# Expert up products from split fp32r parts, and another order of a pair's tiles on TensorE

## The chip, the core and the metric

The kernel runs on one core of a Trainium2 chip. What counts is the device time of one launch in microseconds. The median of three runs before the change is 1347.92 us (1346.98 to 1354.15).

## What is computed

Sixteen sequences of 256 tokens with 256 features pass through three blocks, each with a layer norm ahead and a residual sum behind: attention with its own small feed-forward network, cross attention to a context with another, and a layer of eight experts. The change concerns the last one. Each token goes to the expert whose centroid is nearest, and only this expert's output is kept:

```
xn = rms_norm(x, scale)
ids = argmin(dist2(xn, centroids), axis=-1)
for e in range(8):
    h = xn @ up_w[e]            # (tokens, 256) @ (256, 1024)
    a, g = split(h, 2)
    y = (a * silu(g)) @ down_w[e]   # (tokens, 512) @ (512, 256)
    out = where(ids == e, y, out)
return out + skip
```

Everything is float32 at the ends.

## The kernel before

**Batches.** A first phase runs over the sequences as batches, five stages deep (P, A, B, D, C in `PHASES`): in one turn the stages work on five batches at once. Each engine has its own program, a function `turn(it)` that is run once for each turn, and engines meet by semaphores alone. In the last turns stages fall away: turn B + 1 has B, D and C, turn B + 2 has D and C, turn B + 3 has C alone. Stage D is the second half of cross attention's network (`D.h0` to `D.h3` and `D.out`), stage C normalises its result (`c_x2`), makes the rows for the experts (`c_rows`), stores them to `rows_x` and `rows_skip` and finds each token's expert (`nearest`). In turn B + 1 SyncE also loads the experts' weights (`load_experts`): `up`, 1 MB for each expert, and `down`, half as much.

**Routing.** When the last rows are stored, VectorE sorts the tokens by expert in a chain of some forty steps on the semaphore `s_route`, with a few products on TensorE between. It ends with `sorted_row`, the rows in order of experts, and `tile_expert`, the expert of each tile of 128 rows. There are 39 tiles.

**Tiles.** Two tiles, u = 0 and 1, make a pair k. `tile_steps` runs `step(k, n, nxt, nxt2)` on every engine: the first pair, then a hardware loop of 16 pairs, two pairs written out, and a last single tile. For each tile GpSimd gathers 128 rows (`m_in`), TensorE transposes them (`transpose_in`), ScalarE copies them to `m_xT`; TensorE makes the up product in two halves of 512 columns, two products over C = 2 chunks each (`up_half`), with the rows as the stationary operand and the expert's weights streaming; ScalarE takes SiLU of the gate half (`m_sg`), VectorE multiplies with the other (L1482, `m_h`); TensorE transposes the hidden rows (`turn_hidden`, L1869), ScalarE copies them (L878, `m_hT`), TensorE makes the down product (`down_tile`), VectorE adds the skip rows (`m_out`) and GpSimd scatters the result. TensorE reads the expert's number from `tile_expert` into a register (`value_load`, L1855) and addresses the weights by it.

TensorE's order in a pair is written by hand: the up product of tile 0, the first half of tile 1's, the transposes of tile 0's hidden rows, the second half of tile 1's up product, the down product of tile 0, the transposes of tile 1's hidden rows, the transposes of the next pair's rows, the down product of tile 1.

All products of the experts are in fp32. Other products of the kernel are already made from fp32r parts: a value is rounded to fp32r (`hi`), the rest is taken (`low`), and three passes hi.hi, hi.low and low.hi are summed.

Of the kernel before, what the change touches and what calls it, by code (L numbers as in the profile page):

```python
# [166 lines left out]
def _build(nc, d, ctx):  # L167
# [77 lines left out]

    b_kh, b_kl, b_qh, b_ql = (sbuf(ctx, name, [P, C, S], F32R) for name in ("b_kh", "b_kl", "b_qh", "b_ql"))
# [6 lines left out]
    def carver():  # L253

        at = [0]
# [21 lines left out]
    w1o = p1("w1o", [P, C, D])  # L277
    w11 = p1("w11", [P, C, HID])
    w12 = p1("w12", [P, J, D])
# [8 lines left out]

    rec = p1("rec", [P, 3, S])
    rec_few = p1("rec_few", [P, 16])  # L290
    x1 = p1("x1", [P, T, D])

    c_in = p1("c_in", [P, T, D])
    b_ctxT = p1("b_ctxT", [P, C, S])
    b_xl = p1("b_xl", [P, T, D])
    b_xT = p1("b_xT", [P, C, S])


    b_v = p1("b_v", [P, T, D])
    b_nm = p1("b_nm", [P, T, C, 4, 32])  # L300
    b_p = p1("b_p", [P, NPB, T, S])
    b_zT = p1("b_zT", [P, C, S])
    b_yT = p1("b_yT", [P, C, S])
    b_q = p1("b_q", [P, T, D])
    b_hT = p1("b_hT", [P, J, S])
# [211 lines left out]
    s_route, s_pp, s_wmoe = map(sem, ("routing_chain", "prefixes_made", "experts_loaded"))  # L517
# [13 lines left out]
    pr.close()  # L531
    up = sbuf(ctx, "up", [P, E, C, 2 * EH])
    down = sbuf(ctx, "down", [P, E, EJ, D])
    p3 = carver()
    m_row = p3("m_row", [P, 2, 2, 1], U32)
    m_token = p3("m_token", [P, 2, 1], U32)
    m_in = p3("m_in", [P, 2, D])
    m_skip = p3("m_skip", [P, 2, D])
    m_xT = p3("m_xT", [P, 2, C, P])
    m_sg = p3("m_sg", [P, 2, EH])  # L540
    m_h = p3("m_h", [P, 2, EH])
    m_hT = p3("m_hT", [P, 2, EJ, P])
    m_out = p3("m_out", [P, 2, D])
    oh = p3("oh", [P, NT, E])
    r_pp = p3("r_pp", [P, NT, E])
# [17 lines left out]
    r_id = p3("r_id", [P, 4, TILES_MAX])  # L563
# [9 lines left out]
    BY_TILE = {"m_loaded": 16, "m_skip": 16, "m_row": 1, "m_x": 1, "m_xT": 1, "m_up": 1, "m_silu": 1,  # L573
# [14 lines left out]
    PAIRS = (TILES_MAX - 1) // 2  # L588
# [3 lines left out]
    H_BANK, DOWN_BANK = (6, 2), (7, 4)  # L592

    def tile_steps(eng, body):
        body(0, 2, 2, 2)
        with eng.Fori(0, PAIRS - 3) as k:
            body(k + 1, 2, 2, 2)
        body(PAIRS - 2, 2, 2, TILES_MAX - 2 * PAIRS)
        body(PAIRS - 1, 2, TILES_MAX - 2 * PAIRS, 0)
        if TILES_MAX > 2 * PAIRS:  # L600
            body(PAIRS, 1, 0, 0)

# [4 lines left out]
    def _(sp):  # L607
# [23 lines left out]
        def load_experts():  # L631

            after(sp, "b_xl", B - 1)
            for e in range(E):
                sp.dma_start(up[:, e], w_view(d["L0_ffn_up_w"][e])).then_inc(s_wmoe, 16)
                sp.dma_start(down[:, e], w_view(d["L0_ffn_down_w"][e])).then_inc(s_wmoe, 16)
# [47 lines left out]
    def _(act):  # L684
# [29 lines left out]

        def evacuate(it, job, dst, view=None):

            src = full(act, it, job)[:]
            copy(dst, src if view is None else view(src)).then_inc(e_sem(job), 1)  # L718

        def turn(it):  # L720
# [15 lines left out]
            if Dd:  # L736
                copy(flat(d_qT_hi[:]), full(act, it, "D.q")[:]).then_inc(sig["d_qhi"], 1)
            if A:
# [65 lines left out]
            for what, st, n in PLAN:  # L804
                if st not in it.stages:
                    continue
                if what == "lengths":
                    after(act, "c_rows", c, T)
                    for t in range(T):
                        nc.scalar.activation(b_zT[:, t], c_rows[:, t, 0:D], ACT.Square,  # L810
# [18 lines left out]
            if Cc:  # L829
                for t in range(T):  # L830
                    nc.scalar.activation(c_x2[:, t], c_x2[:, t], ACT.Identity, scale=c_sc[:, 7, t:t + 1],
                                         bias=c_sc[:, 9, t:t + 1]).then_inc(sig["c_rows"], 1)
            if it.first == SPLIT_FROM - 1:
                round_aside((2,))
# [34 lines left out]
        def transposed(k, u):  # L869
            after_tile(act, "m_x", k, u)  # L870
            copy(m_xT[:, u].rearrange("p c s -> p (c s)"), bank[u][:, 0:C * P]).then_inc(mig[u]["m_xT"], 1)

        def step(k, n, nxt, nxt2):
            for u in range(n):
                after_tile(act, "m_up", k, u)
                nc.scalar.activation(m_sg[:, u], bank[3 + 2 * u][:], ACT.Silu).then_inc(mig[u]["m_silu"], 1)  # L876
                after_tile(act, "m_ht", k, u)
                copy(m_hT[:, u].rearrange("p j s -> p (j s)"), bank[H_BANK[u]][:]).then_inc(mig[u]["m_hT"], 1)  # L878
            for u in range(nxt):
                transposed(k + 1, u)  # L880
# [9 lines left out]
    def _(pool):  # L890
# [156 lines left out]

        def step(k, n, nxt, nxt2):
            for u in range(nxt2):
                after_tile(pool, "m_x", k + 1, u)  # L1050
                after_tile(pool, "m_row", k, u)
                gather(m_in, rows_x, m_row[:, 0, u], "m_loaded", u)
            for u in range(n):

                after_tile(pool, "m_out", k, u)
                pool.indirect_dma_start(
                    out=d["out"], out_offset=bass.IndirectOffsetOnAxis(ap=m_token[:, u], axis=0),
                    in_=m_out[:, u], in_offset=None, bounds_check=B * S - 1, oob_is_err=False,
                ).then_inc(mig[u]["m_stored"], 16)
                if u < nxt:  # L1060
                    gather(m_skip, rows_skip, m_row[:, 1, u], "m_skip", u)
# [9 lines left out]
    def _(dve):  # L1071
# [101 lines left out]
        def turn(it):  # L1173
# [155 lines left out]
            if it.first == SPLIT_FROM:  # L1329
                for name in SPLIT[::2]:  # L1330
                    dve.wait_ge(s_low_out[name], 16)
            if Dd:
# [612 lines left out]
```

## Time and profile before

| | us |
|---|---|
| median of three runs | 1347.92 |
| profiled execution | 1350.49 |
| its span, first to last instruction | 1348.8 |
| batches, to 1013 | 1013.0 |
| drain and routing, to the first up product | 72.5 |
| experts, to the end | 263.3 |

The stages are cut by hand at the start of turn B + 2's work and at the first up product. In the profile's rows PE is TensorE, PEld its weight loads, DVE VectorE, ACT ScalarE, POOL GpSimd and SP SyncE; a time is counted from the span's start. An fp32 product appears as two records. The idle time in square brackets is that of the engine just before the row, with what ended it; "issue" means that the engine waited for nothing that the profile shows.

### The profile page before, as it was taken

The page shows a single profiled execution, that of the slowest core. Times are in us where ns is not written, and L with a number is a line of the kernel's source. Part 1 is how long each engine was busy: PE and PEld are TensorE (multiplying, and loading weights), DVE is VectorE, ACT ScalarE, POOL GpSimd, SP SyncE. Part 2 cuts the span into 40 slices and gives each one's busy share as a digit, 9 for nine tenths or more (in the row PEclk, how much of TensorE's full clock was granted, in tenths as well). Part 3 has the DMA queues.
Part 4 walks back from the last instruction along what each step waited for, and adds up shares of the span by engine and source line. Part 5 has one row for each costly group of instructions (what it writes and reads, how often), then busy time and mean ns, then how long its engine had stood idle before and what let it go on. Part 6 is the DMA issues. An engine that isn't in the chain of part 4 may idle for free.

```text
span 1348.8 us, 29314 instructions
## 1 busy us (share of the span) xinstructions
PE 1223.9 (91%) x9542; PEld 915.5 (68%) x9543; DVE 811.2 (60%) x2110; ACT 611.4 (45%) x1288; POOL 413.7 (31%) x712
## 2 busy tenths in 40 slices
PE   6497999999999999999999999999985289999997
PEld 4274778778787877878787787878765145555554
DVE  3737667777786877778687777877644611211211
ACT  3426456464746646474654647465442122222211
POOL 1310324233142423314142331414122234444352
PEclk9598999999999999999999999999998589999998
DMA  8402520303213030321303032130383012121121
GB/s 265 126 1 110 222 107 17 111 16 109 80 52 117 16 109 16 109 80 48 121 16 109 16 109 77 48 124 9 111 324 113 16 49 64 51 62 53 55 66 28
DMA packets 51768, 112.29 MB, mean 83 GB/s; under 512 B 7333, under 2 KB 38863, under 8 KB 44944
## 3 DMA queue, kind: packets, MB, share of 16 engines
q1 hardware_dynamic: 45456, 96.81, 21.3%
q0 software_dynamic: 5616, 14.43, 3.6%
q10 hardware_dynamic: 656, 0.52, 0.1%
q8 instruction: 24, 0.39, 0.1%
q14 instruction: 16, 0.13, 0.0%
HBM read 89.72 MB, written 22.94 MB: 84 GB/s over the span
## 4 chain that ended last, share of the span: by engine, by line
PE 76%; DVE 10%; ACT 6%; issue 5%; DMA 2%; POOL 1%; SPq 0%; DVEq 0%; ACTq 0%; POOLq 0%
PE bank L1505 69%; PE bank L1540 3%; DVE a_p L1295 2%; PE bank L1706 2%; ACT shared L823 2%; PE bank L1869 1%; DMA rows_skip<-shared 1%; ACT shared L878 1%; ACT a_p L818 1%; DVE b_ql L1199 1%; DVE a_split L1227 1%; DVE a_split L1226 1%; DVE a_split L1225 1%; DVE a_ss L1236 1%; ACT a_sq L741 1%
## 5 line engine op out<-in xcount | busy, mean ns | idle before, releaser
L1505 PE MATMUL bank<-shared 128*128 128x256 f32 (+4 forms) x1730 | 320.3, 376 | 27.6 <-POOL shared L1030 11.3
L1505 PEld LDWEIGHTS bank<-shared 128*128 128x128 f32 (+2 forms) x1730 | 219.8, 166 | 88.7 <-issue 31.7
L1295 DVE TENSOR_TENSOR a_p<-a_p,eb 128x385 f32<-128x385 f32 x256 | 125.9, 555 | 75.6 <-ACT a_p L818 75.6
L1505 PE MATMUL bank<-up,shared 128*128 x312 | 143.8, 604 | 11.1 <-issue 11.1
L991 POOL TENSOR_SCALAR a_rz<-a_ms 128x2 f32<-128x2 f32 x16 | 3.1, 191 | 407.5 <-ACT a_sq L842 407.5
L818 ACT ACTIVATE a_p<-bank 128x385 f32<-128x385 f32 x256 | 105.1, 504 | 44.3 <-PE bank L1505 44.2
L1482 DVE TENSOR_TENSOR shared<-bank,shared 128x512 f32<-128x512 f32 x39 | 27.0, 692 | 153.7 <-ACT shared L876 153.7
L1505 PEld LDWEIGHTS bank<-up,shared 128*128 128x128 f32 x312 | 56.9, 192 | 75.6 <-issue 75.6
L876 ACT ACTIVATE shared<-bank 128x512 f32<-128x512 f32 x39 | 23.3, 597 | 137.2 <-PE bank L1505 137.2
L1505 PE MATMUL bank<-down,shared 128*128 x312 | 76.8, 390 | 7.2 <-ACT shared L878 7.2
L823 ACT ACTIVATE shared<-bank 128x512 f32<-128x512 f32 x128 | 66.1, 603 | 35.3 <-PE bank L1505 35.3
L1262 DVE TENSOR_REDUCE shared<-bank 128x2 f32<-128x512 f32 x128 | 79.4, 684 | 1.3 <-PE bank L1505 1.3
L1505 PEld LDWEIGHTS bank<-down,shared 128*128 128x128 f32 x312 | 58.2, 192 | 27.2 <-issue 20.9
L971 POOL TENSOR_TENSOR a_split<-a_sq,a_split 128x256 f16<-128x256 f32 x64 | 42.8, 699 | 104.6 <-ACT a_split L772 104.6
L1035 POOL DMA_INDIRECT shared<-rows_x,shared x35 | 33.1, 945 | 112.1 <-PE bank L1844 107.0
L1505 PE MATMUL bank<-a_p,a_v 128*32 128x256 f32 (+1 forms) x1024 | 58.5, 347 | 8.0 <-DVE a_p L1295 6.2
L1505 PE MATMUL bank<-w_low,a_hT_hi 128*128 128x256 f32 x224 | 63.4, 283 | 0.0
L1505 PE MATMUL bank<-w_hi,a_hT_hi 128*128 128x256 f32 x224 | 62.9, 281 | 0.0
L1505 PE MATMUL bank<-d_qT_hi,w_hi 128*128 128x256 f32 x256 | 57.4, 306 | 5.8 <-DVE d_qT_low L1122 5.8
L1505 PE MATMUL bank<-w_hi,a_hT_low 128*128 128x256 f32 x224 | 62.4, 279 | 0.0
L1505 PE MATMUL bank<-w0qk,a_xnT 128*128 128x512 f32 x128 | 61.1, 621 | 0.7 <-ACT a_xnT L718 0.7
L927 POOL TENSOR_TENSOR shared<-shared,mhalf 128x2 f32<-128x2 f32 x80 | 56.3, 704 | 12.7 <-POOL shared L959 6.6
(237 smaller groups left out, 2724.8 us busy)
## 6 DMA issues: line engine op xcount, KB each, us to landing
w_low<-low_w SPq DMA_DIRECT2D x44, 1024.0 KB, 4.8
up<-in_L_ffn_up_w SPq DMA_DIRECT2D x8, 1024.0 KB, 13.9
x_in<-in_x SPq DMA_DIRECT2D x16, 256.0 KB, 2.7
shared<-in_ctx SPq DMA_DIRECT2D x16, 256.0 KB, 3.1
rows_x<-shared SPq DMA_DIRECT2D x16, 256.0 KB, 5.8
rows_skip<-shared SPq DMA_DIRECT2D x16, 256.0 KB, 6.2
down<-in_L_ffn_down_w SPq DMA_DIRECT2D x8, 512.0 KB, 12.3
toep<-a_hT SPq DMA_DIRECT2D x1, 3072.0 KB, 10.2
```

Of the source, the lines that this page charges most:

```text
L818: nc.scalar.activation(a_p[:, head % NPA], ps[:, 0:SCOLS], ACT.Exp).then_inc(e_sem(f"A.s{head}"), 1)
L823: nc.scalar.activation(b_p[:, head % NPB].rearrange("p t s -> p (t s)"), ps[:], ACT.Exp).then_inc(e_sem(f"B.s{head}"), 1)
L876: nc.scalar.activation(m_sg[:, u], bank[3 + 2 * u][:], ACT.Silu).then_inc(mig[u]["m_silu"], 1)
L927: pool.tensor_tensor(out, in_, mhalf[:, 0:out.shape[-1]], ALU.pow).then_inc(sig[name], 1)
L971: ins = pool.tensor_tensor(a_split[:, t, H0:, slot, :], hat[:, H0:], a_split[:, t, H0:, 0, :], ALU.subtract)
L1035: pool.indirect_dma_start(out=dst[:, u], out_offset=None, in_=src.ap(), in_offset=bass.IndirectOffsetOnAxis(ap=rows, axis=0)).then_inc(mig ...
L1262: dve.tensor_reduce(b_nm[:, n // 4, :, n % 4, 0:1], ps[:].rearrange("p (m s) -> p m s", s=S), AX_X, ALU.max, negate=True).then_inc(e_sem(f ...
L1295: tt(a_p[:, n_ % NPA], a_p[:, n_ % NPA], eb[:, n_], ALU.mult).then_inc(sig["a_p"], 1)
L1482: tt(m_h[:, u], bank[2 + 2 * u][:], m_sg[:, u], ALU.mult).then_inc(mig[u]["m_h"], 1)
L1505: return mm(out, lhsT=lhsT, rhs=rhs, start=first, stop=last, **kw)
L1540: ins = nc.tensor.transpose(ps[:, c * S + t * P:c * S + (t + 1) * P], x[:, t, c * P:(c + 1) * P], ident[:])
L1706: ins = nc.tensor.transpose(ps[:, g * P:(g + 1) * P], a_split[:, t, h:h + 2].rearrange("p h s d -> p (h s d)"), ident16[:])
```

## The change

**Up products.** `up_half` makes six products instead of two: m_xhi with up_hi, m_xhi with up_low, m_xlow with up_hi, each over two chunks, all in fp32r. ScalarE's copy of the transposed rows now writes m_xhi in fp32r, and VectorE gets a new step for each tile, `rest_of_rows`, which subtracts it from the transposed rows in PSUM and writes m_xlow.

**Weights.** `up_hi` is made by ScalarE (`round_up_weights`, eight casts of 128x2048) and `up_low` by VectorE (`rest_of_up`, sixteen subtracts of 128x1024, in place of `up`). ScalarE makes experts 0 to 2 in turn B + 2 after the cast of D.q, 3 to 6 after the same turn's C rows, and 7 once VectorE has taken D.out. VectorE makes the parts of experts 0 to 3 in turn B + 2 before it takes D.out, 4 and 5 after the statistics of c_x2, 6 and 7 at the end of the routing chain. TensorE waits for all of them before the first transposes of rows. Each expert's load has a semaphore of its own. `up_hi` lies where tensors of the first phase lay, and these are laid out in another order.

**Order in a pair.** On TensorE: the whole up product of tile 0, the down product of tile 1 of the pair before, the transposes of tile 0's hidden rows, the transposes of the next pair's tile 0, the whole up product of tile 1, the down product of tile 0, the transposes of tile 1's hidden rows, the transposes of the next pair's tile 1. The expert of the tile before is loaded once more at a pair's start. The other engines' steps follow this order. Two pairs are written out ahead of the loop now, which has 15 turns. Rows of both tiles share bank 0, the down products bank 7.

```diff
+        def round_up_weights(which):
+            for e in which:
+                act.wait_ge(s_up[e], 16)
+                copy(flat(up_hi[:, e]), flat(up[:, e])).then_inc(s_up_hi, 1)
...
+        def rest_of_up(halves):
+            for n in halves:
+                e, c_ = n // C, n % C
+                if c_ == 0:
+                    dve.wait_ge(s_up_hi, e + 1)
+                ins = tt(up_low[:, e, c_], up[:, e, c_], up_hi[:, e, c_].bitcast(F32), ALU.subtract)
+            ins.then_inc(s_up_low, len(halves) // C)
...
+            if it.first == B + 2:
+                rest_of_up(range(0, 8))
             if Dd:
                 ps = full(dve, it, "D.out")
...
+            if it.first == B + 2:
+                rest_of_up(range(8, 12))
...
+        rest_of_up(range(12, 16))
+
+        def rest_of_rows(k, u):
+            after_tile(dve, "m_xT", k, u)
+            tt(flat(m_xlow[:, u]), x_bank(u), flat(m_xhi[:, u]).bitcast(F32), ALU.subtract
+               ).then_inc(mig[u]["m_xl"], 1)
...
-            def up_half(u, half):
-                for c in range(C):
-                    w = up[:, bass.ds(expert[u], 1), c, half * EH:(half + 1) * EH]
-                    ins = product(bank[2 + 2 * u + half][:], m_xT[:, u, c], w.rearrange("p o n -> p (o n)"),
-                                  c == 0, c == C - 1)
+            def up_half(u, half, x_low_new):
+                for x, w_part in ((m_xhi, up_hi), (m_xhi, up_low), (m_xlow, up_hi)):
+                    if x is m_xlow and x_low_new:
+                        after_tile(pe, "m_xl", k, u)
+                    for c in range(C):
+                        w = w_part[:, bass.ds(expert[u], 1), c, half * EH:(half + 1) * EH]
+                        ins = product(bank[2 + 2 * u + half][:], x[:, u, c], w.rearrange("p o n -> p (o n)"),
+                                      c == 0 and x is m_xhi and w_part is up_hi, c == C - 1 and x is m_xlow)
                 return ins
...
+            choose(0, 2 * k)
+            if further:
+                choose(-1, 2 * k - 1)
+            up_tile(0)
+            if further:
+                down_tile(1, 1)
             if n == 2:
+                choose(1, 2 * k + 1)
             turn_hidden(0)
+            if nxt > 0:
+                transpose_in(k + 1, 0)
             if n == 2:
+                up_tile(1)
+            down_tile(0, 0)
             if n == 2:
                 turn_hidden(1)
-            for u in range(nxt):
-                transpose_in(k + 1, u)
-            if n == 2:
-                down_tile(1)
+            if nxt > 1:
+                transpose_in(k + 1, 1)
```

TensorE at the end of the pair loop, before (ISA rows set addresses, TENSOR_LOAD reads an expert's number; the rows behind the branch are the next pair, and a loop turn begins with the same two loads):

```order
L1505 ISA
L1505 MATMUL bank<-down,shared 128x256
L596 REGISTER_ALU
L596 COMPARE_AND_BRANCH
L1855 TENSOR_LOAD tile_expert
L1855 ISA x2
L1855 TENSOR_LOAD tile_expert
L1855 ISA x2
L1505 ISA [waits m_hT1,m_h0,m_xT0]
L1505 MATMUL bank<-up,shared 128x512
```

The same place after:

```order
L1962 MATMUL bank<-ident,shared 128x128 [waits m_hT1,m_h1]
L1962 MATMUL bank<-ident,shared 128x128 x3
L1929 MATMUL bank<-ident,shared 128x128 [waits m_xl0,m_loaded1]
L1929 MATMUL bank<-ident,shared 128x128
L616 REGISTER_ALU
L616 COMPARE_AND_BRANCH
L1940 TENSOR_LOAD tile_expert
L1940 ISA x2
L1940 TENSOR_LOAD tile_expert
L1940 ISA x2
L1589 ISA [waits m_h0,m_xT0]
L1589 MATMUL bank<-up_hi,m_xhi 128x512
```

The down products of tile 1 stood between the last wait and the branch; now the transposes of tile 1's hidden rows and of the next rows stand there.

VectorE in turn B + 2, from the end of `nearest` (CAST expert_of) to the statistics of stage D's result, before (L1335 takes D.out):

```order
L1194 CAST expert_of<-shared 128x2 [waits c_index]
L1335 TENSOR_TENSOR shared<-bank,shared 128x512 [waits b_qb2,bank_full5]
L1134 BN_STATS shared<-shared 128x6 [waits bank_free5]
L1134 BN_STATS shared<-shared 128x6
L1137 BN_AGGR shared<-shared 128x2 [waits c_stats] x2
```

After, from the last of the eight subtracts on (L1390 takes D.out):

```order
L1163 TENSOR_TENSOR up_low<-up,up_hi 128x1024 [waits up_weights_rounded]
L1163 TENSOR_TENSOR up_low<-up,up_hi 128x1024
L1390 TENSOR_TENSOR shared<-bank,shared 128x512 [waits b_qb2,bank_full5]
L1187 BN_STATS shared<-shared 128x6 [waits bank_free5]
L1187 BN_STATS shared<-shared 128x6
L1190 BN_AGGR shared<-shared 128x2 [waits c_stats] x2
```

Eight rows like the first two stand between the CAST and the row that takes D.out.

VectorE at the end of turn B + 2, from the statistics of c_x2 to the first step of turn B + 3, which waits for GpSimd's chain of norms, before:

```order
L1134 BN_STATS shared<-shared 128x6 [waits c_x2]
L1134 BN_STATS shared<-shared 128x6
L1137 BN_AGGR shared<-shared 128x2 [waits c_stats2] x2
L1269 SCALAR_TENSOR_TENSOR shared<-shared 128x256 [waits c_norms]
L1269 SCALAR_TENSOR_TENSOR shared<-shared 128x256
```

After, from the last row of the statistics on:

```order
L1190 BN_AGGR shared<-shared 128x2 [waits c_stats2] x2
L1163 TENSOR_TENSOR up_low<-up,up_hi 128x1024 [waits up_weights_rounded]
L1163 TENSOR_TENSOR up_low<-up,up_hi 128x1024
L1163 TENSOR_TENSOR up_low<-up,up_hi 128x1024 [waits up_weights_rounded]
L1163 TENSOR_TENSOR up_low<-up,up_hi 128x1024
L1322 SCALAR_TENSOR_TENSOR shared<-shared 128x256 [waits c_norms]
```

Four subtracts stand between the statistics, for which GpSimd's chain of norms waits, and the step that waits for this chain.

## Rows read from the trace of the kernel before

**Rows 1.** Busy time in two stretches (stretch, us, busy by engine, granted clock, DMA).
```profile
1013.00:1085.50 72.50, 27.97 (x160) 22.65 (x158) 34.79 (x96) 13.02 (x31) 21.94 (x43) 0.67 0.16 58
1085.50:1348.80 263.30, 239.60 (x854) 141.79 (x854) 50.27 (x189) 57.06 (x116) 109.92 (x113) 0.98 0.18 53
```

**Rows 2.** Timeline, TensorE, one pair in the loop (start, duration, work, idle before).
```profile
1283.67 5.41 PE L1505 MATMUL bank<-up,shared 128*128 x12 [0.63 <-issue]
1288.92 0.60 PE L1869 MATMUL bank<-ident,shared 128*128 128x128 f32 x4
1289.36 1.88 PE L1505 MATMUL bank<-up,shared 128*128 x4
1291.08 1.89 PE L1505 MATMUL bank<-down,shared 128*128 x8
...
1294.16 1.99 PE L1505 MATMUL bank<-down,shared 128*128 x8 [0.33 <-ACT shared L878]
1296.79 5.41 PE L1505 MATMUL bank<-up,shared 128*128 x12 [0.64 <-issue]
```

**Rows 3.** Timeline, TensorE, fp32r products of batch work, eight steps apart.
```profile
560.06 0.28 PE L1505 MATMUL bank<-w_hi,a_hT_hi 128*128 128x256 f32 x1
...
561.00 0.28 PE L1505 MATMUL bank<-w_hi,a_hT_low 128*128 128x256 f32 x1
```

**Rows 4.** Timeline of a pair's second half: products, multiply, weight loads (PEld).
```profile
1107.42 1.89 PE L1505 MATMUL bank<-down,shared 128*128 x8
...
1108.25 0.69 DVE L1482 TENSOR_TENSOR shared<-bank,shared 128x512 f32<-128x512 f32 x1 [3.18 <-ACT shared L876]
...
1108.99 0.51 PEld L1869 LDWEIGHTS bank<-ident,shared 128*128 128x128 f32 x4
...
1110.50 1.59 PEld L1505 LDWEIGHTS bank<-down,shared 128*128 128x128 f32 x8 [0.56 <-issue]
...
1113.19 0.30 PEld L1505 LDWEIGHTS bank<-up,shared 128*128 128x128 f32 x2 [1.10 <-issue]
```

**Rows 5.** Timeline, TensorE, written-out pairs and the last tile.
```profile
1319.92 1.99 PE L1505 MATMUL bank<-down,shared 128*128 x8 [0.33 <-ACT shared L878]
1321.91 5.41 PE L1505 MATMUL bank<-up,shared 128*128 x12
...
1340.66 3.15 PE L1505 MATMUL bank<-down,shared 128*128 x8 [0.76 <-ACT shared L878]
```

**Rows 6.** Timeline, TensorE's weight loads before the first up product.
```profile
1083.83 0.29 PEld L1844 LDWEIGHTS bank<-ident,shared 128*128 128x128 f32 x2 [0.79 <-DMA shared<-rows_x,sorted_row]
...
1085.49 0.50 PEld L1505 LDWEIGHTS bank<-up,shared 128*128 128x128 f32 x2 [1.37 <-issue]
```

**Rows 7.** Groups by shape: cast and subtract of 2048 columns (busy us, mean ns).
```profile
L713 ACT CAST made<-w 128x2048 fp32r<-128x2048 f32 x1 | 1.9, 1930 | 0.0
...
L1111 DVE TENSOR_TENSOR made<-w,made 128x2048 fp32r<-128x2048 f32 x1 | 2.3, 2325 | 1.2 <-DMA rounded_w<-made 1.2
```

**Rows 8.** Loads of up weights: last issue (SyncE), and sizes, us to landing.
```profile
1002.38 3.26 SPq L635 DMA_DIRECT2D up<-in_L_ffn_up_w  x1
...
up<-in_L_ffn_up_w SPq DMA_DIRECT2D x8, 1024.0 KB, 13.9
```

**Rows 9.** Timeline of the drain: ScalarE once, VectorE twice.
```profile
1027.36 0.47 ACT L754 ACTIVATE shared<-bank,shared 128x256 f32<-128x256 f32 x1 [8.12 <-PE bank L1505]
...
1041.38 0.69 DVE L1335 TENSOR_TENSOR shared<-bank,shared 128x512 f32<-128x512 f32 x1 [4.22 <-PE bank L1505]
...
1050.68 0.88 DVE L1269 SCALAR_TENSOR_TENSOR shared<-shared 128x256 f32<-128x256 f32 x2 [3.80 <-POOL shared L955]
```

**Rows 10.** Timeline of the drain, GpSimd and VectorE at the same time.
```profile
1027.47 1.31 POOL L980 TENSOR_TENSOR shared<-shared 128x512 f32<-128x512 f32 x1
...
1027.55 2.96 DVE L1269 SCALAR_TENSOR_TENSOR shared<-shared 128x256 f32<-128x256 f32 x2 [3.20 <-POOL shared L955]
```

More of the change, by code:

```diff
@@ L737, in turn @@
                 copy(flat(d_qT_hi[:]), full(act, it, "D.q")[:]).then_inc(sig["d_qhi"], 1)
+            if it.first == B + 2:
+                after(act, "x1_kept", B - 1)
+                round_up_weights(range(3))
             if A:
@@ L832, in turn @@
                                          bias=c_sc[:, 9, t:t + 1]).then_inc(sig["c_rows"], 1)
+            if it.first == B + 2:
+                after(act, "c_nx", c)
+                round_up_weights(range(3, E - 1))
+                taken(act, it, "D.out")
+                round_up_weights(range(E - 1, E))
             if it.first == SPLIT_FROM - 1:
@@ L1046, in _, with store, next_rows @@
             gather(m_in, rows_x, sorted_row[:, 2 + u:3 + u], "m_loaded", u)
-        def step(k, n, nxt, nxt2):
[L1049 to L1061, printed above, removed]
+        def store(k, u, n, more):
+            after_tile(pool, "m_out", k, u, n)
+            pool.indirect_dma_start(
+                out=d["out"], out_offset=bass.IndirectOffsetOnAxis(ap=m_token[:, u], axis=0),
+                in_=m_out[:, u], in_offset=None, bounds_check=B * S - 1, oob_is_err=False,
+            ).then_inc(mig[u]["m_stored"], 16)
+            if more:
+                gather(m_skip, rows_skip, m_row[:, 1, u], "m_skip", u)
+        def next_rows(k, u):
+            after_tile(pool, "m_x", k + 1, u)
+            after_tile(pool, "m_row", k, u)
+            gather(m_in, rows_x, m_row[:, 0, u], "m_loaded", u)
+        def step(k, n, nxt, nxt2):
+            if not isinstance(k, int) or k > 0:
+                store(k, 1, 0, n == 2)
+            if nxt2 > 0:
+                next_rows(k, 0)
+            store(k, 0, 1, nxt > 0)
+            if nxt2 > 1:
+                next_rows(k, 1)
         tile_steps(pool, step)
@@ new lines, in next_row, with hidden_tile, sum_out @@
+        def next_row(k, u):
+            after_tile(dve, "m_loaded", k + 1, u)
+            ts(m_row[:, 0, u], of_tile(3, 2 * k + 4 + u), 1.0, None, ALU.mult).then_inc(mig[u]["m_row"], 1)
+        def hidden_tile(k, u):
+            after_tile(dve, "m_silu", k, u)
+            tt(m_h[:, u], bank[2 + 2 * u][:], m_sg[:, u], ALU.mult).then_inc(mig[u]["m_h"], 1)
+        def sum_out(k, u, back, more):
+            after_tile(dve, "m_stored", k, u, -back)
+            ts(m_token[:, u], of_tile(2, 2 * k + u - 2 * back), 1.0, None, ALU.mult)
+            after_tile(dve, "m_down", k, u, 1 - back)
+            after_tile(dve, "m_skip", k, u, 1 - back)
+            if more:
+                ts(m_row[:, 1, u], of_tile(3, 2 * k + 2 + u - 2 * back), 1.0, None, ALU.mult)
+            tt(m_out[:, u], down_bank(u), m_skip[:, u], ALU.add).then_inc(mig[u]["m_out"], 1)
```

189 lines of the change are left out of this document (101 added, 88 removed).

## The prediction

> **What bounds the kernel now.** I read the busy time by stage first, then TensorE's rows of one pair of tiles, then the rows of the stage between the last batch and the first tile. From 1085.50 on, the experts take 263.30 us and TensorE is busy for 239.60 of them at a granted clock of 0.98, while VectorE is busy for 50.27 and ScalarE for 57.06 [rows 1]: this stage is TensorE's, and shorter products there shorten it. The 72.50 us before it (the drain) are different: TensorE is busy for 27.97, VectorE for 34.79, no engine is full [rows 1], and the end is set by a chain of small dependent steps in which VectorE takes part. Work added there on VectorE costs time wherever it outlasts VectorE's wait.
>
> A pair takes 1296.79 - 1283.67 = 13.12 us [rows 2]. The reader is to see two holes in it: 0.33 us before the second down product (waiting for ScalarE's copy) and 0.64 us, called issue, before the next pair. An up product of 512 columns is two records of 0.43 us (1.72 us for four, from 1289.36 to 1291.08), so a tile's four take 3.44; a down product of a tile takes the same 1.72, four transposes 0.44 (1288.92 to 1289.36) [rows 2].
>
> **The up products.** They go from four fp32 products to twelve fp32r products of 512 columns a tile. The trace has fp32r products of 256 columns only: eight steps from 560.06 to 561.00 are 0.1175 us each [rows 3]. For 512 columns the upper bound is twice that, 0.235. The lower one is half an fp32 record of the same 512 columns, 0.215 [rows 2]. A part of the 0.1175 may belong to the instruction and not to its columns, and no row tells how much, so I take the middle, 0.225: 12 x 0.225 = 2.70 us a tile against 3.44. The bounds are 2.58 and 2.82.
> The 256-column step is longer than a rule gives: the Trainium skill, "TensorE: Matmul & The Clock Gate", section "Back-to-back issue gap", states N/2.4 + 2.5 ns, thus 109 ns for 256 columns and 216 for 512, and does not speak of fp32r. The row's 117.5 decides for 256. An estimate by that page's 216 ns would make a tile 2.59 us and the whole kernel some 4 us shorter than my sum.
>
> **The order in a pair.** A whole up product now stands ahead of the down product of the tile before it, and this covers the way from an up product through SiLU and the multiply to the transposes of the hidden rows: its end at 1107.42, VectorE's multiply at 1108.25, the weight load of the transposes at 1108.99, thus 1.57 us [rows 4], under a down product of 1.72. That hole stays closed, and the 0.33 us before the second down product goes, since the copy of m_hT has a whole up product as cover.
>
> What is late next is the pair's end. The 0.64 us there is not TensorE's array but its sequencer: released at 1110.50 by m_hT, it issues four down products, the branch and two loads of an expert's number, and only 2.69 us later, at 1113.19, the next up product's weights [rows 4]. Where the steps are written out without a loop, the down product starts at 1319.92 and the up product at 1321.91, 1.99 apart instead of 2.63 with no idle left [rows 5]: the branch is worth 0.64, and the two loads hide only because 1.72 us of down products are queued behind the wait. In the new order the last wait before the branch is on m_h of tile 1, and behind it are queued only its four transposes and two of rows, 0.44 + 0.22 = 0.66 us. So from the end of the second up product it takes 1.57 to the wait's release and then some 2.69 (six transposes for four down products, the rest the same): 4.26 us, where the array has 1.72 + 0.66 = 2.38 to do. The hole at the pair's end grows from 0.64 to 1.88 us.
> The third load of an expert's number stands behind the down product of the tile before, which the sequencer issues early since its waits are long over; I cost it at nothing, and at up to 0.83 us a pair if that is wrong (two loads with two transposes take 1085.49 - 1083.83 = 1.66 [rows 6]).
>
> A pair in the loop after: 2.70 + 1.72 + 0.66 + 2.70 + 4.26 = 12.04, against 13.12: 1.08 x 15 loop turns = 16.2 us. The new step 1 is written out and takes 12.04 - 0.64 = 11.40 against 13.12; the two pairs after the loop take 11.40 against some 12.4: 1.7 + 2.0 = 3.7. The first pair has two shorter up products (2 x 0.74 = 1.5), the single last tile one (0.74), and its down product, which took 3.15 us instead of 1.99 with TensorE idle before it [rows 2, 5], should lose these 1.16, since the down product of the tile before now fills that idle time: 3.4 together. Sum of the experts' stage: **23.3 us saved**. VectorE and ScalarE get one subtract and none respectively more per tile; at a fifth of their time busy [rows 1] this costs nothing, and GpSimd's six transfers a pair keep their number.
>
> **The drain.** Eight casts of 128x2048 at 1.93 us on ScalarE, sixteen subtracts of 128x1024 on VectorE, each half of 2.33, so 1.17 us [rows 7]. The last load of up weights is issued at 1002.38 and a load lands 13.9 us after its issue [rows 8], before any of them is needed. Three casts (5.8 us) go into ScalarE's idle 8.12 us that end at 1027.36 [rows 9]: nothing. The other five follow the C rows, when ScalarE waits anyway: nothing, else a few us if VectorE had to wait for one.
> The subtracts come in three places. Eight stand ahead of the add that takes D.out: 9.4 us where VectorE idled 4.22 [rows 9]: **+5.2**. Behind them wait that add, the statistics and everything to the routing. Four come after the statistics of x2: 4.7 us where VectorE idles 3.80 [rows 9], at least +0.9. But GpSimd runs its ten-step chain of norms in that idle time, and the trace shows the two in each other's way: two VectorE operations with both inputs in SBUF took 2.96 us while GpSimd multiplied rows from SBUF [rows 10], and the same two 0.88 at 1050.68 without [rows 9]. If the four and the chain can't overlap, it costs all 4.7; I take **+4.4**. The last four follow sorted_row and TensorE waits for them before the first transposes: from 1079.3 to 1084.0, then rows 0, their low part, rows 1 and one load; the first transposes of the second rows stood at 1083.83 [rows 6]. I count **+1.3** at the first up product, and up to +5.3 if GpSimd's gathers and the subtracts hold each other up.
> The Trainium skill's "SBUF — State Buffer", section "Who interferes with whom", agrees with the rows at 1027.55 (a VectorE instruction with two SBUF inputs contends with a GpSimd one that reads SBUF), but infers that a tensor_tensor does not hold up the writing of descriptors. By this rule the gathers run on and the 5.3 falls away; no row of before shows it.
> Sum of the drain: 5.2 + 4.4 + 1.3 = **10.9 us lost**, bounds 7.4 and 15.2.
>
> **Sum.** The profiled execution took 1350.49 us (span 1348.8), 2.6 above the median 1347.92; the sum is made in its rows: 1350.49 - 23.3 + 10.9 = 1338.1, and against the median 1335.5. With the bounds of the product (4.7 us either way over 39 tiles) and of the drain this case reaches from 1327 to 1345.
>
> **The rivals.**
> *The hole at the pair's end does not grow*, because the sequencer gets through loads and branch faster when it isn't behind products. For it: the hole is only 0.64 now. Against it: 2.69 us from release to load with nothing else to do [rows 4]. It gives 1.24 us back in each of 19 pairs, 23.6: 1312.
> *The third load is not covered*: 0.83 x 19 = 15.8 us more: 1351, no change. For it: loads are long [rows 6]; against it: the down product before it has no open wait.
> *Slower: the sequencer can't feed the array.* Each up tile needs twenty sequencer steps now (twelve products, eight address steps) against eight. From 1110.50 to 1113.19 it made seventeen in 2.69 us, 0.16 each [rows 4]; at that price a tile takes 3.2 us instead of 2.70, over 39 tiles 19.5 us more: 1355. It turns the gain into a loss from 3.02 us a tile on. Against it: those seventeen hold the loads and the branch, and fp32r products with fixed addresses come every 0.1175 [rows 3].
> *Slower: the clock falls in the hole.* After the idle times of the last tile the down product ran 3.15 us against 1.99 [rows 2, 5]. If each of 19 holes did that, it would cost 1.16 x 19 = 22: 1357. Against it: a hole of 1.88 us stands between stretches without idle time, while there two lay close together.
>
> **How the numbers follow.** Forecast 1335.5 with chance 0.61; the hole that doesn't grow 0.13; the third load 0.14; fed too slowly 0.08; clock 0.04. Half a per cent, what a measurement of this kernel can tell from no change, is 6.7 us: 1341.2 to 1354.7. Of the forecast's own range about a sixth lies above 1341.2. Faster 0.51 + 0.13 = 0.64; same 0.10 + 0.14 = 0.24; slower 0.12. The range runs from 1312 to 1352, leaving out half of the first rival and the two slower ones, under 2 in 10.
>
> **What would show it.** In the loop, twelve up products in 2.6 to 2.8 us, no idle time before the hidden transposes, an issue hole of 1.7 to 2.0 us before each pair and a pair of 11.8 to 12.3. In the drain, the add of D.out some 5 us later, GpSimd's chain of norms stretched, the first up product some 11 us later. An issue hole under 1 us or up products over 3 us a tile would make the prediction wrong.

## The result, and the profile after

The changed kernel takes 1334.95 us (median of 4 runs, 1334.41 to 1335.46), the kernel before 1347.45 on the same chip (1346.82 to 1354.15): 12.5 us by the two medians. The ratio of the runs is 0.9888 (95% interval 0.987 to 0.9906), which is 15.1 us (12.7 to 17.5). The medians probably understate the gain: in the experiments below, the kernel before has medians of 1349.1 to 1350.5 from 7 to 11 runs. The forecast was 1335.5. The profiled execution took 1335.46 (span 1333.7), 15.0 less than that of before, which was 3 us above its own median; the traces are compared with each other below, stage by stage, since the batches' work ahead of the drain differs by several us between executions.

The two stretches of [rows 1], at the same times after the change (stretch, us, busy by engine, granted clock, DMA):

```profile
1013.00:1085.50 72.50, 27.27 (x156) 22.89 (x156) 46.50 (x101) 26.31 (x36) 20.14 (x38) 0.67 0.15 56
1085.50:1334.00 248.50, 209.23 (x1017) 173.56 (x1014) 73.29 (x240) 58.30 (x118) 116.18 (x117) 0.97 0.20 58
```

VectorE's busy time in the drain rose from 34.79 to 46.50 us, ScalarE's from 13.02 to 26.31: the splitting of the weights. The drain now ends at 1095.18, so the second row still holds its last 9.7 us. In the experts' stage alone, from 1095.18 on, TensorE is busy for 207.72 of 238.52 us: its work fell from 239.60, but it is idle for 30.8 us where it was idle for 23.7. What it waits for there, after and (second fence) before (waited for, us in total, times, longest):

```profile
PE bank L1589 <- issue: 24.2, 20, 1.4
...
PE bank L1589 <- ACT shared L913: 0.8, 1, 0.8
```
```profile
PE bank L1505 <- issue: 11.1, 18, 1.0
PE bank L1505 <- ACT shared L878: 7.2, 20, 0.8
```

The 20 waits for ScalarE's copy are gone all but the last one, and the idle time called issue has more than doubled. One pair in the loop, which answers to [rows 2] (TensorE: start, duration, work, idle before; then weight loads, PEld, of its second half):

```profile
1203.62 0.73 PE L1589 MATMUL bank<-up_hi,m_xhi 128*128 x2 [1.41 <-issue]
...
1206.46 1.89 PE L1589 MATMUL bank<-down,shared 128*128 x8
1208.18 0.60 PE L1962 MATMUL bank<-ident,shared 128*128 128x128 f32 x4
1208.62 0.38 PE L1929 MATMUL bank<-ident,shared 128*128 128x128 f32 x2
1208.76 0.71 PE L1589 MATMUL bank<-up_hi,m_xhi 128*128 x2
1209.31 0.63 PE L1589 MATMUL bank<-up_low,m_xhi 128*128 x2
...
1211.61 1.89 PE L1589 MATMUL bank<-down,shared 128*128 x8
...
1215.57 0.72 PE L1589 MATMUL bank<-up_hi,m_xhi 128*128 x2 [1.42 <-issue]
```
```profile
1213.18 0.51 PEld L1962 LDWEIGHTS bank<-ident,shared 128*128 128x128 f32 x4
1213.66 0.25 PEld L1929 LDWEIGHTS bank<-ident,shared 128*128 128x128 f32 x2
1215.57 0.32 PEld L1589 LDWEIGHTS bank<-up_hi,m_xhi 128*128 128x128 f32 x2 [1.65 <-issue]
```

The pair takes 1215.57 - 1203.62 = 11.95 us (13.12 before). Twelve up products take 2.85 (1208.76 to 1211.61): two of 512 columns every 0.46, but the first two 0.55. No idle time stands before the transposes of the hidden rows, and one hole of 1.41 ends the pair.

The drain, VectorE, then GpSimd, which answers to [rows 9, 10]:

```profile
1037.62 9.17 DVE L1163 TENSOR_TENSOR up_low<-up,up_hi 128x1024 fp32r<-128x1024 f32 x8
1046.70 0.69 DVE L1390 TENSOR_TENSOR shared<-bank,shared 128x512 f32<-128x512 f32 x1
...
1052.12 4.60 DVE L1163 TENSOR_TENSOR up_low<-up,up_hi 128x1024 fp32r<-128x1024 f32 x4
1058.93 0.88 DVE L1322 SCALAR_TENSOR_TENSOR shared<-shared 128x256 f32<-128x256 f32 x2 [2.21 <-POOL shared L990]
...
1087.58 4.63 DVE L1163 TENSOR_TENSOR up_low<-up,up_hi 128x1024 fp32r<-128x1024 f32 x4
```
```profile
1052.29 1.10 POOL L968 TENSOR_SCALAR shared<-shared 128x2 f32<-128x2 f32 x1 [2.80 <-DVE shared L1190]
1053.47 1.53 POOL L962 TENSOR_TENSOR shared<-shared,mhalf 128x2 f32<-128x2 f32 x1
1055.08 0.55 POOL L972 TENSOR_TENSOR shared<-shared 128x2 f32<-128x2 f32 x1
1055.71 1.06 POOL L974 TENSOR_TENSOR shared<-shared 128x2 f32<-128x2 f32 x1
...
1087.85 2.08 POOL L1070 DMA_INDIRECT shared<-rows_x,sorted_row  x1 [6.52 <-DVE sorted_row L1530]
1090.24 1.67 POOL L1070 DMA_INDIRECT shared<-rows_x,sorted_row  x1 [0.31 <-issue]
```

VectorE no longer idles ahead of the D.out add. Beside four subtracts the first four steps of GpSimd's chain of norms took 1.10, 1.53, 0.55 and 1.06 us (0.22, 0.70, 0.20 and 0.20 before), and the two gathers beside the last four took 2.08 and 1.67 (1.25 and 0.96 before). The first up product follows at 1095.18.

To compare drains whatever came before them, I count from VectorE's subtract of D's q, a step that the change left as it was (before at 1023.67, after at 1024.24). Added by the change: 4.75 us up to the D.out add (17.71 to 22.46), 2.93 from there to the last batch's rows (9.30 to 12.23), nothing in the routing, 1.42 from the list of rows to the first up product (6.40 to 7.82): 9.1. From the first up product to the end: 263.3 us before, 238.5 after, 24.8 saved.

### The profile page after: what moved, and what is told of

Its sections match the earlier page's. It is cut to its first block, busy times and chain, and to the rows that moved or that the text cites. A ratio compares the mean times of both kernels' runs of the same rounds, so it can differ in the third digit from the quotient of the medians.

```text
span 1333.7 us, 29945 instructions
## 1 busy us (share of the span) xinstructions
PE 1192.6 (89%) x9698; PEld 948.7 (71%) x9699; DVE 846.5 (63%) x2165; ACT 625.9 (47%) x1296; POOL 417.6 (31%) x712
## 4 chain that ended last, share of the span: by engine, by line
PE 75%; DVE 11%; issue 6%; ACT 5%; DMA 2%; POOL 1%; SPq 0%; DVEq 0%; ACTq 0%; POOLq 0%
PE bank L1589 67%; PE bank L1624 3%; DVE a_p L1348 2%; PE bank L1790 2%; ACT shared L852 2%; PE bank L1962 1%; DVE up_low L1163 1%; DMA rows_skip<-shared 1%; ACT a_p L847 1%; PE bank L1929 1%; DVE b_ql L1252 1%; DVE a_split L1279 1%; DVE a_split L1280 1%; DVE a_ss L1289 1%; DVE a_split L1278 1%
## 5 line engine op out<-in xcount | busy, mean ns | idle before, releaser
L911 ACT ACTIVATE shared<-bank 128x512 f32<-128x512 f32 x39 | 23.3, 597 | 113.0 <-PE bank L1589 113.0
L1589 PE MATMUL bank<-up_hi,m_xhi 128*128 x156 | 53.1, 422 | 24.2 <-issue 24.2
L1589 PE MATMUL bank<-down,shared 128*128 x312 | 73.8, 379 | 0.8 <-ACT shared L913 0.8
L1086 POOL DMA_INDIRECT out_rows<-shared x39 | 39.5, 1012 | 98.0 <-DVE shared L1562 90.7
L962 POOL TENSOR_TENSOR shared<-shared,mhalf 128x2 f32<-128x2 f32 x80 | 57.2, 715 | 12.7 <-POOL shared L994 6.6
L882 ACT ACTIVATE a_hT_hi<-bank 128x512 fp32r<-128x512 f32 x56 | 33.5, 598 | 52.9 <-PE bank L1589 52.9
## 6 DMA issues: line engine op xcount, KB each, us to landing
down<-in_L_ffn_down_w SPq DMA_DIRECT2D x8, 512.0 KB, 12.4
toep<-a_hT SPq DMA_DIRECT2D x1, 3072.0 KB, 10.2
```

Of the source, the lines that this page charges most:

```text
L882: nc.scalar.activation(flat(a_hT_hi[:, 2 * n:2 * n + 2]), ps[:], ACT.Relu).then_inc(sig["a_hhi"], 1)
L962: pool.tensor_tensor(out, in_, mhalf[:, 0:out.shape[-1]], ALU.pow).then_inc(sig[name], 1)
L1086: pool.indirect_dma_start(out=d["out"], out_offset=bass.IndirectOffsetOnAxis(ap=m_token[:, u], axis=0), in_=m_out[:, u], in_offset=None, b ...
L1589: return mm(out, lhsT=lhsT, rhs=rhs, start=first, stop=last, **kw)
```

## The experiments

A turning is the transposes of a tile's hidden rows h; the loop's turn is the branch back to its head. Theory S: TensorE's sequencer makes the hole at the pair's end. The last wait ahead of the branch and the two loads of expert numbers is answered late, and little is queued behind it. Rival A: the hole is a wait for another engine. For the drain, theory D: the 9 us are subtracts in VectorE's chain; theory C: subtracts and GpSimd's work slow each other.

**The turned loop.** TensorE's loop body now begins ahead of the pair's last turning, so that branch and loads run while a down product is queued:

```
+                turn_hidden(1, 1)
+                if n == 2:
+                    transpose_in(k, 1)
             up_tile(0)
...
             down_tile(0, 0)
-            if n == 2:
-                turn_hidden(1)
-            if nxt > 1:
-                transpose_in(k + 1, 1)
```

> Only TensorE's program changes: the loop's turn is moved from behind the pair's last turning (turn of h 1, tile k+1's second input) to ahead of it, so that the branch and the two loads of expert numbers are executed while the down product of tile 0 still runs. Theory S (the 1.41 us hole at each pair's end is TensorE's sequencer: branch and two register loads behind the last wait): the loop's pair falls from 11.96 us to 10.5 to 10.7, the written-out pairs lose their 0.7, together 15 x 1.41 + 4 x 0.7 = 24 us, time 1309 to 1314. Rival A (the hole is the wait for an answer of ScalarE or VectorE, which comes no earlier): pair stays at 11.9 to 12.0, time 1333 to 1337. Between them: the loads are hidden but the turning now waits for h, a hole of 0.3 to 0.8 stays, 1316 to 1325.

Measured: 1307.26 us, ratio to before 0.9676 (0.966 to 0.9692). The pair fell to 10.31 us: the weight loads of the turning and of the next up product stand 0.63 us apart instead of 2.39. Time and pair lie a little under the bands of S: a pair lost 1.64 us, not 1.41, since the up product now also starts before the record of the transposes ends (1204.33, 1204.58). TensorE at the pair's end, then its weight loads there and the next pair's, then a stretch of 140 us (columns as in [rows 1]):

```profile
1202.04 1.89 PE L1589 MATMUL bank<-down,shared 128*128 x8
1203.76 0.60 PE L1962 MATMUL bank<-ident,shared 128*128 128x128 f32 x4
1204.20 0.38 PE L1929 MATMUL bank<-ident,shared 128*128 128x128 f32 x2
1204.33 0.71 PE L1589 MATMUL bank<-up_hi,m_xhi 128*128 x2
```
```profile
1203.68 0.44 PEld L1962 LDWEIGHTS bank<-ident,shared 128*128 128x128 f32 x4 [0.16 <-issue]
...
1204.31 0.30 PEld L1589 LDWEIGHTS bank<-up_hi,m_xhi 128*128 128x128 f32 x2
...
1213.99 0.44 PEld L1962 LDWEIGHTS bank<-ident,shared 128*128 128x128 f32 x4 [0.16 <-issue]
```
```profile
1150.00:1290.00 140.00, 140.00 (x707) 118.27 (x707) 46.43 (x161) 39.50 (x82) 80.17 (x82) 1.00 0.25 74
```

TensorE is busy for 140.00 of 140.00 us. Rival A falls: no answer came earlier, only instructions moved on one engine.

**The loop written out**, on TensorE alone:

```
-        tile_steps(pe, step)
+        for k in range(PAIRS - 2):
+            step(k, 2, 2, 2)
...
```

> Only TensorE's program changes: its 15 loop turns are written out, the other engines keep their loops. Theory S: the branch goes, the two loads of expert numbers stay behind the last wait, so the hole falls from 1.41 us to the 0.7 of the pairs that are written out already; 15 x 0.7 = 10.5 us, time 1323 to 1327. Rival A (an answer is awaited): unchanged, 1333 to 1337. Rival F (15 pairs of new code have to be fetched, and TensorE waits for that): slower than 1337.

Measured: 1325.36 us, ratio 0.982 (0.9801 to 0.9839); experts' stage 228.3 us, 10.2 less than after the change. The hole that is left:

```profile
1206.38 0.73 PE L1589 MATMUL bank<-up_hi,m_xhi 128*128 x2 [0.68 <-issue]
```

The loop's turn is worth 1.41 - 0.68 = 0.73 us of the hole. The rest I put down to the two loads behind the wait; no run takes both away at this place. The Trainium skill, "Advanced Engine Details and Errata", section "Control Flow Timing", gives some 108 ns for a compare-and-branch; the 0.73 us here hold more than that, what else in the turn no run here parts. No wait for code shows (rival F).

**The order alone, and the passes alone.**

```
-                for x, w_part in ((m_xhi, up_hi), (m_xhi, up_low), (m_xlow, up_hi)):
...
+                for c in range(C):
+                    w = up[:, bass.ds(expert[u], 1), c, half * EH:(half + 1) * EH]
...
```

> The new order alone: whole up product, down product of the tile ahead, turning, with the up products in fp32 as before, no split rows, and no rounding or subtracting of weights in the drain. Theory S: the pair's work without holes is that of before, 13.12 - 0.97 = 12.15 us, and the hole at its end is the 1.41 of now: pair 13.4 to 13.7, so the order alone costs 0.3 to 0.5 a pair and the time is 1353 to 1358. Rival O (the order is what brings the gain, the hand-offs are what cost): pair 12.1 to 12.5, time 1328 to 1336. Both: first up product at 1085 to 1086, where it stood before.

Measured: 1350.26 us, ratio 1.0007 (0.9992 to 1.0023); pair 13.31 us, hole 1.41. Nearer to S than to O, and both missed: the order costs 0.2 a pair in the trace, and nothing that the times can tell. The first up product came at 1084.23, just ahead of its band.

```profile
1204.82 3.70 PE L1569 MATMUL bank<-up,m_xhi 128*128 x8 [1.41 <-issue]
```

The other half (the drain's work and the passes stay, and TensorE's sequence, the banks and the other engines' steps are those of before):

```
+                up_half(1, 1, True)
             turn_hidden(0)
...
             if n == 2:
...
+                up_half(1, 0, False).then_inc(mig[1]["m_up"], 1)
+            down_tile(0)
...
```

> Three fp32r passes and the drain's work as now, with the order and banks of before (both expert numbers loaded at the head, half of tile 1's up product on either side of the turning of h 0, both input tiles turned ahead of the down product of tile 1). Theory S: the pair's work falls to 11.96 - 1.41 = 10.55 us; the hole at the end is the 0.64 of before, the hole ahead of the turning of h 0 grows from 0.33 to 0.65 as its cover is 0.3 us shorter: pair 11.7 to 12.0, time 1330 to 1336, so the order was worth nothing. Rival O (the order is needed to cover the hand-offs): pair over 12.4, time over 1343.

Measured: 1338.28 us, ratio 0.9902 (0.9881 to 0.9922), an interval that overlaps the full change's; pair 12.05, with the two holes of [rows 2] as they were. Its pair lies 0.05 and its time 2 us above the bands of S, and the hole ahead of the turning of h 0 that I had feared did not open: the 0.32 stands ahead of the second down product.

```profile
1202.50 1.99 PE L1581 MATMUL bank<-down,shared 128*128 x8 [0.32 <-ACT shared L912]
1205.13 0.72 PE L1581 MATMUL bank<-up_hi,m_xhi 128*128 x2 [0.64 <-issue]
```

So nearly all of the gain comes from the passes: by the ratios they alone bring 13.2 us, the whole change 15.1. The order gave some 2 us by the ratios and 3.3 by the medians, and the intervals overlap.

**What the order is worth with the turned loop.** The passes with the order of before and the loop turned at the same place, three loads at its head (against the kernel of the passes alone):

```
             for u in range(n):
                 choose(u, 2 * k + u)
+            if not isinstance(k, int) or k > 0:
+                choose(-1, 2 * k - 1)
+                turn_hidden(1, 1)
+                for u in range(n):
+                    transpose_in(k, u)
+                down_tile(1, 1)
...
```

> Three passes, the order of work of before, and TensorE's loop turned as in the first experiment: branch and three loads of expert numbers stand ahead of the pair's last turning. It asks what the new order is worth once the sequencer's hole is gone. Theory W (the order was worth little only because its own hole at the turn ate it): the pair falls from 12.05 us by the 0.66 hole and some 0.2 of restart to 11.1 to 11.3, the 0.32 hole ahead of the last down product stays, time 1322 to 1326, so that the order is worth 15 us or more beside the turned loop's 1307. Rival N (the order is worth nothing, holes of 0.3 apart): pair 10.3 to 10.7, time 1307 to 1314.

Both missed: 1341.43 us, ratio 0.9927 (0.9908 to 0.9946), pair 12.07. The hole moved ahead of the turning. ScalarE's copy of h 0, VectorE's multiply for h 1, and TensorE's weight loads:

```profile
1200.62 0.59 ACT L912 COPY shared<-bank 128x512 f32<-128x512 f32 x1 [1.47 <-PE bank L1949]
...
1202.62 0.69 DVE L1548 TENSOR_TENSOR shared<-bank,shared 128x512 f32<-128x512 f32 x1 [2.75 <-ACT shared L910]
...
1201.57 1.71 PEld L1581 LDWEIGHTS bank<-down,shared 128*128 128x128 f32 x8
1204.40 0.42 PEld L1949 LDWEIGHTS bank<-ident,shared 128*128 128x128 f32 x4 [1.12 <-issue]
```

The multiply ended at 1203.31, the turning began 1.1 us later. But the down product in front could be issued only from the copy's end at 1201.21, and from there the sequencer had eight products, the branch and three loads to do. Two more kernels test this (theory Q). One moves a load from the head of this loop behind tile 0's up product; the other has three loads at the head in the new order. The edit of the first, against the kernel just shown:

```
-            for u in range(n):
-                choose(u, 2 * k + u)
+            choose(0, 2 * k)
...
             if n == 2:
+                choose(1, 2 * k + 1)
```

> The kernel of the run before last (passes, order of before, turned loop) with one of its three loads at the loop's head, that of tile 1's expert, moved behind tile 0's up product. There the turning of h 1 began at 1204.40 us, though h had been written by 1203.3 and the down product of tile 0 could be issued only from ScalarE's copy at 1201.21. Theory Q (from that copy on TensorE's sequencer issues 8 products, then the branch and the loads, then the turning: it is late by its own work): one load fewer brings the turning 0.4 to 0.6 us sooner, pair 11.4 to 11.7 instead of 12.07, time 1331 to 1335. Rival (something else holds the turning): pair 12.0 to 12.1, time 1339 to 1343.

> The turned loop with the new order, and all three loads of expert numbers at its head instead of two. Theory Q: here the wait ahead of the loads, for the copy of h 0, is answered by 1199.83 us, 3.8 us before the turning, so the sequencer has some slack: the third load adds 0 to 0.3 us to the 0.16 us hole, pair 10.3 to 10.6, time 1306 to 1313. Rival (loads at the head cost their full price wherever the last wait lies): pair 10.7 to 10.9, time 1315 to 1319.

Measured: 1324.59 us (ratio 0.982, 0.9796 to 0.9843) and 1308.25 (0.97, 0.9676 to 0.9724). In the old order one load fewer brought the pair from 12.07 to 11.29, a little more than expected (the time lies 6 us under the band of Q), and the turning is then released by VectorE; in the new order the third load costs nothing, pair 10.31, wait unchanged. Weight loads of the first and its next down product, then weight loads of the second:

```profile
1203.45 1.71 PEld L1581 LDWEIGHTS bank<-down,shared 128*128 128x128 f32 x8
1205.51 0.42 PEld L1949 LDWEIGHTS bank<-ident,shared 128*128 128x128 f32 x4 [0.34 <-DVE shared L1548]
...
1206.92 1.99 PE L1581 MATMUL bank<-down,shared 128*128 x8 [0.32 <-ACT shared L912]
```
```profile
1207.34 0.44 PEld L1962 LDWEIGHTS bank<-ident,shared 128*128 128x128 f32 x4 [0.16 <-issue]
```

From the down product's first load to the turning's it is 2.83 us with three loads and 2.06 with two: a load of an expert's number with its address steps is worth 0.77 us or more where it isn't covered. With the loop turned and two loads at its head, the new order is 1324.6 - 1307.3 = 17 us faster than the old. The idle time that is left in the old order is no longer the sequencer's but that of hand-offs: 0.34 us for VectorE's multiply and 0.32 for ScalarE's copy in the rows above. The new order covers both, and no idle time of TensorE shows in its stretch of 140 us.

**The subtracts spread.** In the drain, 16 subtracts in VectorE's waits: 2, 2 and 3 up to the D.out add, none beside the norms, 1, 2, 1 and 2 after, 3 behind the list of rows.

```
+                if it.first == B + 2:
+                    rest_of_up(range(0, 2))
...
-                rest_of_up(range(0, 8))
+                rest_of_up(range(4, 7))
...
-                rest_of_up(range(8, 12))
```

> Only the places of VectorE's 16 subtracts in the drain change: 2 and 2 into the two waits for the last-but-one batch's distances, 3 instead of 8 ahead of D.out, none where GpSimd makes the norms, 1 and 2 into the last batch's waits, 1 ahead of the routing, 2 into its wait for the prefixes, 3 instead of 4 behind the list of rows. Theory D (the drain's 9 us are subtracts that stand in VectorE's chain where something waits for it): the cost of place 1, 4.8 us, and of place 2, 2.9 us, falls to under 1 together, place 3 keeps about 1: the first up product comes 7.5 to 8.5 us sooner and the time is 1326 to 1329. Rival L (the drain is longer for another reason, ScalarE's roundings or the up weights' transfer): 1332 to 1337. Theory C (a subtract and GpSimd's work slow each other): GpSimd's norms of the last batch take the 0.70, 0.21 and 0.20 us of before again; the two gathers that run beside the last 3 subtracts still take 1.5 to 2.1 us instead of 1.0 to 1.25.

Measured: 1327.63 us, ratio 0.9824 (0.9785 to 0.9862). Counted as above the drain is 8.1 us shorter than after the change and 1.0 longer than before, as theory D says, and rival L falls; the D.out add and the last batch's rows stand 17.72 and 9.30 us behind their marks, as before the change. VectorE idles there again, and GpSimd's multiply has its old time; the gathers do not:

```profile
1043.42 0.69 DVE L1398 TENSOR_TENSOR shared<-bank,shared 128x512 f32<-128x512 f32 x1 [0.53 <-PE bank L1597]
1052.72 0.88 DVE L1330 SCALAR_TENSOR_TENSOR shared<-shared 128x256 f32<-128x256 f32 x2 [3.81 <-POOL shared L990]
```
```profile
1049.31 0.70 POOL L962 TENSOR_TENSOR shared<-shared,mhalf 128x2 f32<-128x2 f32 x1
...
1081.71 2.08 POOL L1070 DMA_INDIRECT shared<-rows_x,sorted_row  x1 [6.52 <-DVE sorted_row L1538]
1084.10 1.67 POOL L1070 DMA_INDIRECT shared<-rows_x,sorted_row  x1 [0.31 <-issue]
```

**Turned loop and another spread:** the 3 from behind the list of rows go beside the norms.

```
+            if it.first == B + 2:
+                rest_of_up(range(7, 10))
...
-        rest_of_up(range(13, 16))
```

> The turned loop together with a second spread: as in the first spread up to D.out (2, 2, 3), then 3 subtracts in the wait for GpSimd's norms, 1 and 2 in the last batch's waits, 1 ahead of the routing, 2 in its wait for the prefixes, none behind the list of rows. Theory S and D together: the turned loop's 1307 less 8 us, 1297.5 to 1301. Theory C: the gathers, with no subtract beside them, take 1.0 to 1.25 us, and the first transposes come 5.4 us or a little less after the list of rows, as before the change, not 6.8; the 3 subtracts beside the norms cost 0.5 to 1.5 us there. Rival (no contention: beside the norms they are hidden, and the gathers last as long as with the subtracts): norms at their old times, gathers at 1.7 to 2.1 us.

Measured: 1299.42 us, ratio 0.9639 (0.9592 to 0.9685). The two contentions changed places, as C says: the multiply takes 1.53 us again, the three subtracts cost 2.08 there (more than the 0.5 to 1.5 expected), and the gathers run free, 6.40 us from list of rows to first up product, to the hundredth what it was before the change.

```profile
1044.03 3.46 DVE L1163 TENSOR_TENSOR up_low<-up,up_hi 128x1024 fp32r<-128x1024 f32 x3
...
1045.38 1.53 POOL L962 TENSOR_TENSOR shared<-shared,mhalf 128x2 f32<-128x2 f32 x1
...
1078.95 1.25 POOL L1070 DMA_INDIRECT shared<-rows_x,sorted_row  x1 [6.51 <-DVE sorted_row L1540]
1080.51 0.96 POOL L1070 DMA_INDIRECT shared<-rows_x,sorted_row  x1 [0.31 <-issue]
```

**Turned loop and the first spread,** one subtract moved ahead:

```
-        rest_of_up(range(10, 11))
+        rest_of_up(range(10, 12))
         phase1_over(dve)
```

> The turned loop with the first spread of the subtracts (none beside the norms), of which one more is moved from behind the list of rows into the waits ahead of the routing: 2 there, 2 in the wait for the prefixes, 2 behind the list of rows. Theories D and C: against the turned loop with the second spread the norms give 2.1 us back and the gathers beside the 2 subtracts cost 0.5 to 0.9, so 1 to 1.6 us less in the trace and 1297 to 1300 by the clock; from list of rows to first up product 6.8 to 7.3 us. Rival L: no different from the second spread.

Measured: 1298.45 us, ratio 0.9611 (0.9595 to 0.9627), the fastest by the median, but its ratio lies within the interval of the run before. In the trace the drain is 0.8 us shorter, not 1 to 1.6: from the list of rows to the first up product it takes 7.46, above the band, so two subtracts there still cost 1.06, about as much as three (0.94).

## Why the prediction was right, point by point

**The up products:** 2.85 us a tile, not 2.70, and 0.03 above the upper bound. A step of 512 columns is 0.23 and not 0.225, near the bound of [rows 3]; the first two products after a turning take 0.55 instead of 0.46, which no term held and which is more than half of the 0.15.

**The order in a pair:** the hand-off is covered as said; from the end of the second up product to the turning it is again 1.57 us (1211.61 to 1213.18). From there to the next up product it is 2.39, not 2.69 [rows 4], and six transposes take 0.58, not 0.66. So the hole is 1.41, under the 1.7 to 2.0 that I named, and the pair comes out right (11.95 for 12.04) because 2 x 0.15 too little and 0.30 + 0.08 too much nearly cancel, which is luck. The cause named for the hole, the sequencer behind a late wait, is shown by the turned loop. The branch at 0.64 [rows 5] measured 0.73. The third load is covered, and its price uncovered, up to 0.83, is at least 0.77.

**The experts' stage:** 24.8 us saved, 23.3 forecast; the last tile's down product fell from 3.15 to 1.99.

**The drain:** 9.1 us lost, 10.9 forecast. Place 1 4.75 for 5.2 (a subtract takes 1.15 us and not 1.17, which is 0.2 of the difference); place 3 1.42 for 1.3; place 2 is the term mis-sized, 2.93 for 4.4. I had let the subtracts and the norms not overlap at all; four subtracts stretched only the first four steps of GpSimd's chain, and VectorE then still waited 2.21 us for the rest. The Trainium skill's "SBUF — State Buffer", section "Who interferes with whom", infers that a tensor_tensor doesn't hold up the writing of descriptors; here the two gathers took 2.08 and 1.67 us beside subtracts and 1.25 and 0.96 without. So the prediction's reading of it, that the gathers run on, fails. The inference itself stays open: a gather also reads its row numbers from `sorted_row`, and no run here parts this from the writing of descriptors. How much of the 1.5 us counts in the changed kernel is open too, since the first transposes wait there for the subtracts; in the first spread, where they wait for the gathers, 0.94 us was lost. The 5.3 that I bounded it with never came near.

**Net:** 15.7 us in the traces (12.4 forecast), less 0.6 by which the profiled execution of after was late before the drain; 12.5 by the medians and 15.1 by the ratio. The saving was forecast 1.5 us too low and the loss 1.8 too high, which add up to 3.3 in the same direction. That the median was met to 0.6 us all the same is luck.

**The rivals:** the sequencer feeds the array (2.85 us a tile, under the 3.02 at which it turns, and TensorE busy throughout in the turned loop); the hole did grow, from 0.64 to 1.41, and it doesn't lower the granted clock, which is 1.00 (2.4 GHz) in the loop of the changed kernel (columns as in [rows 1]):

```profile
1200.00:1320.00 120.00, 107.18 (x532) 89.74 (x530) 35.28 (x122) 29.61 (x61) 58.09 (x60) 1.00 0.22 63
```

## What to carry to other kernels

Look for the last wait ahead of a loop's turn and for when it is answered: branch and register loads cost what the queued work behind that wait does not cover, and moving the turn to a place where the wait is long answered and a product is queued was worth more than the change itself (27.7 us by the medians, against 12.5 to 15.1). A cheaper operation on the bounding engine doesn't have to wait for this: the passes alone, with both holes as they were, brought 1.07 us a pair, where two tiles' up products got 1.18 shorter. The holes are a second gain. Extra work on an engine of a dependent chain goes into its waits in small pieces, and not beside another engine's work that it slows: spread so, 16 subtracts cost 1.0 us instead of 9.1.

## What the runs showed that I had not expected

- Gathers issued by GpSimd took 2.08 and 1.67 us beside VectorE's subtracts with two SBUF inputs, 1.25 and 0.96 where the subtracts had been moved away.
- It goes the other way as well: two subtracts took 3.46 us where the first of them met GpSimd's multiply of 512 columns, and 2.36 elsewhere in the same trace (the first spread):

```profile
1032.22 1.48 POOL L1021 TENSOR_TENSOR shared<-shared 128x512 f32<-128x512 f32 x1
...
1032.47 3.46 DVE L1163 TENSOR_TENSOR up_low<-up,up_hi 128x1024 fp32r<-128x1024 f32 x2
```

- A turn at the same place of the program, with three loads behind it, left a wait of 0.16 us ahead of the turning in one order (pair 10.31 us) and of 1.12 in the other (12.07). The sequencer's work behind the wait for the copy is the same, and the copy ended 3.85 us before the turning in one and 3.19 in the other. The pairs differ by more than this, since the old order also waits for hand-offs.
